# Window attention pass on one core: second norm centred in SBUF, values in the single PSUM bank, 49 weight columns, second MLP product in three parts

## The chip, the cores and the metric

The kernel runs on 1 of the 8 cores of one Trainium2 chip. The metric is device time in microseconds (us). All times are of whole executions of the program on the chip; the profile is one execution under the hardware profiler. The engines are named as in the profile: PE (TensorE; PEld is its weight loads), DVE (VectorE), ACT (ScalarE), POOL (GpSimd) and SP (SyncE, which issues the DMAs). TensorE's clock is granted at one of two levels here, 1.2 and 2.4 GHz; the profile shows the granted share (0.5 or 1).

## The reference

Two residual blocks on x of shape (32, 96, 56, 56), f32: a depthwise 31x31 convolution of the group norm of x, then a vision transformer block on shifted 7x7 windows of the group norm of that.

```python
x = x + conv31x31_depthwise(group_norm(x), weight) + bias_term
x = x + window_block(group_norm(x))

def _ln(x, s, b):
    m = jnp.mean(x, axis=-1, keepdims=True)
    v = jnp.var(x, axis=-1, keepdims=True)
    return (x - m) * jax.lax.rsqrt(v + EPS) * s + b

def _vit(t, ...):                    # t: (windows, 49 tokens, 96), 12 heads of 8
    h = _ln(t, ln1_s, ln1_b)
    q, k, v = h @ wq + bq, h @ wk + bk, h @ wv + bv
    scores = jnp.einsum('nqhd,nkhd->nhqk', q, k) / np.sqrt(dh)
    attn = jax.nn.softmax(scores, axis=-1)
    o = jnp.einsum('nhqk,nkhd->nqhd', attn, v).reshape(N, S, D)
    t = t + o @ wo + bo
    h = _ln(t, ln2_s, ln2_b)
    return t + jax.nn.gelu(h @ w1 + b1) @ w2 + b2
```

The change touches only how the second norm, the values, the product of probabilities and values, and the product with `w2` are placed and ordered.

## The kernel before

`conv_pass` does the first block and writes x1 to DRAM; the change leaves it alone. `window_pass` does the second. Its unit is a **strip**: 8 windows, that is 392 tokens (NT), with the 96 channels on partitions. There are 256 strips (32 images of 8). The pass is a pipeline written out by hand: each engine has one function `step(i, s)` that is unrolled 256 + 9 times, and in one step (one **turn** below) each stage works on another strip: QKV (first norm, q, k, v) on strip n - 2, ATT (scores) on n - 4, SOFT (probabilities) on n - 6, PROJ (attention output and second norm) on n - 7, MLPS on n - 8. The order of an engine's work is the order of the lines of its `step`; semaphores (`S[...]`) tie the engines together. There is no scheduler.

PSUM has eight banks: `ps_s` and `ps_t` two each (scores, transposed scores), `ps_pv` one, `ps_xc` one ("the single bank"), and a ring of two, `ps_ring`. The table `USES` gives the order in which products take the ring's banks; a product may start when the use two places ahead has been read (`wait_bank`, L599). So in the kernel before, the second variance (`var2`) waits for `q_done`, the values (`v`) for `k_done`, and so on.

What PE does in a turn, in order (L1125 to L1190): transposed scores 0 (`below_max`, L1098); the first norm's centring product into `ps_xc` (L1133, L1134); scores 0; transposed scores 1; `times_v` for two window pairs (L1107); `expand` 0 and 1, the first MLP product (L1058 to L1060); scores 1, transposed scores 2, `expand` 2; four transposes of the attention output (L1149); scores 2; the first variance (`spread`, L1066, L1067); the output projection `wo` (L1049); `times_v` for the other two pairs; scores 3; **the centring product of the second norm** into `ps_xc` (L1163, f32); q and k (L1049); transposed scores 3; the transpose of the row maxima (`max_rows`, L1095); **the second variance** as two single-pass products of the squares split in two (`sq2_hi`, `sq2_lo`); **the values** (L1180) into a ring bank; and **the second MLP product** (L1188), nine matmuls, three for each of three blocks of 128 hidden units.

An f32 product is two records in the trace (two weight loads, two matmuls); one in F32R is one record, and where F32R is used an operand is split into a high part and a remainder.

`times_v` multiplies, for each head and window pair, the probabilities as weights with the values as the moving side (two windows of 9 columns: 8 values and a column of ones that yields the denominator). Two window pairs go to the two halves of the partitions. It loads 64 weight columns (`WS`) of which 49 (`TOK`) are tokens; the other 15 are the start of the next head's:

```python
to = ps_pv[WS * odd:WS * odd + WS, ...][:, half, :, h, :]
ins = pe.matmul(to, pt[:, p, at:at + WS], vd[:, m % VR, p, h, :, :], start=True, stop=True,
                skip_group_check=True)
```

The second norm is a chain over three engines: centring product (PE, L1163) into the single bank; two squares (ACT, L848, `sq2` and `sq2_hi`); their difference (DVE, L978, `sq2_lo`); variance (PE); logarithm and exponential (ACT, L827, L832); `h2_hi` and `h2` as product of the single bank with `rstd` (DVE, L1004, L1008); and their difference `h2_lo` (DVE, L1026), which signals `h2_split` and lets `expand` start in the next turn. The single bank is held from the centring product until both products have read it, and the next strip's first norm waits for that (L1130, L1131). On DVE the q and k remainders (L983, L987) stand between L978 and L1004, and the copy of the values (L1014) and the sum `y` (L1021) between L1008 and L1026. POOL splits the hidden units (`mid_high`, `mid_low`: L739, L746), splits the q and k remainders into planes (L788, L792), and adds `y` to the input (L801).

## Time and profile before

| | us |
|---|---|
| median of 3 runs | 5706.78 |
| lowest, highest | 5679.43, 5709.63 |
| the profiled execution, its own time | 5688.4 |
| its span, first to last instruction | 5686.6 |
| PE busy (share of the span) | 5342.2 (94%) |
| DVE, ACT, POOL busy | 3397.2, 3542.0, 3509.3 |
| mean granted clock of TensorE | 0.976 |

How to read it: busy time is summed over instructions, and PE's matmuls are pipelined, so an engine that shows as busy need not be at its peak. The conv pass takes about the first quarter of the span. A row of the groups gives line, engine, operation, output and inputs, shapes (partitions x elements), count, then busy us and mean ns of one, then idle time of the engine just before and what ended it.

### The profile page before, as it was taken

To read this page: it belongs to the slowest core of one execution; us is meant where nothing else is said; L and a number is where in the kernel's file an instruction comes from. 1 tells how busy PE (TensorE), PEld (TensorE's weight loads), DVE (VectorE), ACT (ScalarE), POOL (GpSimd) and SP (SyncE) were. 2 spreads that over 40 slices of the span, in tenths; PEclk is the share of its full clock that TensorE was granted. 3 is DMA by queue.
4 is the path that set the end of the run, shared out by engine and by line. 5 is a ranking of instruction groups with operands and counts; after the bars stand their busy time and mean duration, and the time that the engine had idled before them with its cause. 6 is when DMAs were issued, how large, how long until landed. Compare 5 with 4: busy or idle time off the path is not lost.

```text
span 5686.6 us, 229687 instructions
## 1 busy us (share of the span) xinstructions
PE 5342.2 (94%) x97360; PEld 4217.5 (74%) x97360; DVE 3397.2 (60%) x5850; ACT 3542.0 (62%) x5590; POOL 3509.3 (62%) x4814
## 2 busy tenths in 40 slices
PE   6999999999599999999999999999999999999998
PEld 6999999999466666666666666666666666666665
DVE  2333333433267677677676777776677777777773
ACT  3444444444367777777776777777777777777775
POOL 2222222222367777777777777777777777777774
PEclk9999999999689999999998999999999999999996
DMA  4444444444356666666665666666666666666662
GB/s 125 116 121 120 127 121 120 116 125 104 71 126 140 140 140 140 140 140 140 140 140 127 139 139 140 140 140 140 140 140 140 140 140 140 140 140 140 140 140 47
DMA packets 1099823, 740.58 MB, mean 130 GB/s; under 512 B 465428, under 2 KB 1070708, under 8 KB 1098708
## 3 DMA queue, kind: packets, MB, share of 16 engines
q1 hardware_dynamic: 1069620, 687.18, 53.6%
q0 software_dynamic: 29184, 38.71, 3.2%
q8 instruction: 774, 12.68, 1.0%
q14 instruction: 245, 2.01, 0.1%
HBM read 409.02 MB, written 316.46 MB: 128 GB/s over the span
## 4 chain that ended last, share of the span: by engine, by line
PE 61%; issue 7%; DVE 3%; ACT 3%; POOL 0%; ACTq 0%; DVEq 0%; POOLq 0%
PE ps_pv L1121 14%; PE ps_ring L1188 8%; PE ps_s L1075 5%; PE ps_ring L1058 4%; PE ps_xc L1163 4%; PE ps_ring L1049 4%; PE ps_t L1075 4%; PE ps_ring L1180 4%; PE ps_ring L1066 4%; PE ps_ring L1060 2%; PE ps_ring L1059 2%; DVE b_rest L983 2%; ACT b_sq_hi L848 2%; PE ps_ring L1149 2%; PE ps_ring L1067 2%
## 5 line engine op out<-in xcount | busy, mean ns | idle before, releaser
L940 DVE TENSOR_REDUCE b_mx<-ps_s 113x12 f32<-113x588 f32 x1024 | 783.9, 766 | 200.6 <-PE ps_s L1075 200.4
L1121 PEld LDWEIGHTS ps_pv<-b_vd,b_probs_t 128*64 128x64 f32 x24576 | 771.1, 140 | 164.0 <-issue 155.1
L840 ACT ACTIVATE b_probs_t<-ps_t 128x588 f32<-128x588 f32 x1024 | 667.7, 652 | 303.0 <-PE ps_t L1075 302.9
L225 POOL TENSOR_SCALAR xn<-xin,aff 96x896 f32<-96x896 f32 x192 | 173.4, 903 | 1072.2 <-DVE aff L375 1059.5
L1121 PE MATMUL ps_pv<-b_vd,b_probs_t 128*64 128x18 f32 x24576 | 822.5, 213 | 0.3 <-issue 0.3
L746 POOL TENSOR_TENSOR b_mid_lo<-b_mid,b_mid_hi 128x392 fp32r<-128x392 f32 x768 | 788.9, 1027 | 43.3
L410 PE MATMUL ps_conv<-blocks_hi,toep_hi 128*128 128x288 f32 (+2 forms) x2880 | 667.2, 313 | 0.0
L410 PE MATMUL ps_conv<-blocks_hi,toep_lo 128*128 128x288 f32 (+2 forms) x2880 | 654.4, 309 | 0.0
L410 PE MATMUL ps_conv<-blocks_lo,toep_hi 128*128 128x288 f32 (+2 forms) x2880 | 653.7, 308 | 0.0
L801 POOL TENSOR_TENSOR b_outs<-b_y,b_xs 96x392 f32<-96x392 f32 x256 | 316.7, 1237 | 445.2 <-DVE b_y L1021 445.2
L282 ACT ACTIVATE toep_hi<-toep 128x640 fp32r<-128x640 f32 x288 | 197.2, 749 | 632.9 <-PE ps_conv L410 616.7
L855 ACT ACTIVATE b_mid<-ps_ring,b_cols 128x392 f32<-128x392 f32 x768 | 438.2, 587 | 196.2 <-PE ps_ring L1060 180.5
L827 ACT ACTIVATE b_lg<-ps_ring,b_cols 96x392 f32<-96x392 f32 x512 | 298.4, 583 | 324.8 <-PE ps_ring L1067 321.8
L788 POOL TENSOR_SCALAR b_planes<-b_rest 96x784 bf16<-96x784 f32 x256 | 215.5, 842 | 440.3 <-DVE b_rest L987 440.3
L327 DVE TENSOR_SCALAR conv_sb<-ps_conv,biasb 128x896 f32<-128x896 f32 x96 | 110.5, 1151 | 625.4 <-PE ps_conv L410 625.4
L410 PEld LDWEIGHTS ps_conv<-blocks_hi,toep_lo 128*128 128x128 f32 x2880 | 464.5, 189 | 4.2
L410 PEld LDWEIGHTS ps_conv<-blocks_hi,toep_hi 128*128 128x128 f32 x2880 | 464.4, 189 | 3.9
L410 PEld LDWEIGHTS ps_conv<-blocks_lo,toep_hi 128*128 128x128 f32 x2880 | 464.0, 189 | 4.3
L1075 PEld LDWEIGHTS ps_t<-b_q_st,b_k_st 51*49 51x49 bf16 x24576 | 260.0, 100 | 258.1 <-issue 228.6
L848 ACT ACTIVATE b_sq<-ps_xc 96x392 f32<-96x392 f32 x512 | 252.6, 493 | 312.8 <-PE ps_xc L1163 312.8
L792 POOL TENSOR_TENSOR b_planes<-b_rest,b_planes 96x784 bf16<-96x784 f32 x256 | 432.2, 1688 | 21.3
L739 POOL TENSOR_SCALAR b_mid_hi<-b_mid 128x392 fp32r<-128x392 f32 x768 | 396.5, 516 | 13.0 <-ACT b_mid L855 13.0
(142 smaller groups left out, 12423.3 us busy)
## 6 DMA issues: line engine op xcount, KB each, us to landing
stacked_qk<-b_planes SPq DMA_DIRECT2D x512, 220.5 KB, 2.9
b_q_st<-stacked_qk SPq DMA_DIRECT2D x512, 220.5 KB, 4.3
b_k_st<-stacked_qk SPq DMA_DIRECT2D x512, 220.5 KB, 5.6
toep<-filters_padded SPq DMA_DIRECT2D x96, 936.5 KB, 14.0
stacked_qk<-b_planes SPq DMA_DIRECT2D x512, 147.0 KB, 2.4
stacked_qk<-b_planes SPq DMA_DIRECT2D x512, 73.5 KB, 1.9
b_xs<-x_scratch SPq DMA_DIRECT2D x224, 147.0 KB, 2.8
out<-b_outs SPq DMA_DIRECT2D x224, 147.0 KB, 3.2
```

The costliest lines, as they stand in the source:

```text
L410: ins = pe.matmul(to[:, first // 2:first // 2 + n, y0 * BATCH:y1 * BATCH], taps[:, par, 1 + dy, NDX // 2 + dx, :], data[:, par, first + dx ...
L739: pool.tensor_scalar(mid_hi[:, m, :], mid[:, m, :], 1.0, 0.0, ALU.mult, ALU.add).then_inc(S["mid_high"], 1)
L746: pool.tensor_tensor(mid_lo[:, m, :], mid[:, m, :], mid_hi[:, m, :].bitcast(F32), ALU.subtract).then_inc(S["mid_split"], 1)
L792: pool.tensor_tensor(planes[:, 2, :, :], rest[:, :, :], planes[:, 1, :, :], ALU.subtract).then_inc(S["qk_split"], 1)
L801: pool.tensor_tensor(tokens(outs[:, sl % 2]), windows(y[:, sl % 2, :]), tokens(xs[:, mlps % XS]), ALU.add).then_inc(S["added"], 1)
L840: act.activation(pt[:, p, 0:HEADS * TOK].rearrange("k (e n) -> k e n", e=2), ps_t[:, :, 0:HPAIR * TOK], ACT.Exp, scale=float(DH) ** -0.5). ...
L848: act.activation(dst[:, :], ps_xc[0:C, 0:NT], ACT.Square, scale=scale).then_inc(S[done], 1)
L855: act.activation(mid[:, m, :], bank(i, s, use)[:, 0:NT], ACT.Gelu_apprx_tanh, bias=cols[:, B1 + m:B1 + m + 1]).then_inc(S["gelu_done"], 1)
L940: dve.tensor_reduce(mx[0:rows_q, :].rearrange("q (e m p) -> q e m p", e=2, p=PAIRS)[:, :, :, p], ps_s[0:rows_q, :, 0:HPAIR * TOK].rearrang ...
L1075: ins = pe.matmul(dst[WS * w:WS * w + TOK, e, h * TOK:(h + 1) * TOK], a[k, m % SR, h, t], b[k, m % SR, h, t], start=True, stop=True, skip_ ...
L1121: ins = pe.matmul(to, pt[:, p, at:at + WS], vd[:, m % VR, p, h, :, :], start=True, stop=True, skip_group_check=True)
L1188: ins = pe.matmul(bank(i, s, "w2")[0:C, 0:NT], w[:, m, :], src[:, m, :], start=(m == 0 and n == 0), stop=(m == NM - 1 and n == 2))
```

## The change

- Second norm: PE now forms the **mean** of `t1` (a product with a constant matrix of 1/96) in a ring bank (`mean2`), and DVE subtracts it from `t1` into a new tile `xc2` in SBUF. One square (ACT, of `xc2`) takes the place of two, `sq2_lo` and its DVE instruction are gone, and the variance is one f32 product with `ones_f`. `h2_hi` and `h2` are products of `xc2` and `rstd`, both in SBUF. In DVE's order `xc2` stands ahead of the fourth row maximum.
- Values: their product goes into the single bank `ps_xc`, which holds the first norm's centred values until `h1` is made, and the copy out of it now comes ahead of `h2_hi` on DVE. The next strip's first norm waits for that copy (`v_done`) in place of `h2_high` and `h2_done`. The ring's order changes: `mean2` takes a place ahead of q, `v` has none; the product with `w2` now follows `var2`.
- `times_v` loads 49 weight columns and writes 49 rows. `ps_pv` is set to 1 once at the start, so that the rows between are defined.
- The product with `w2` is `contract`, called for one block of hidden units at a time at the start of the **next** turn: before transposed scores 0, after them, and after the first norm's product.
- On PE the values come ahead of `var2`. On ACT the fourth exponential comes ahead of the second norm's logarithm.

The file of the changed kernel holds two definitions of `window_pass`; the second replaces the first and alone runs, so its lines carry numbers some 650 higher. The diff is that of the function that runs (declarations left out).

```diff
                 ("var1", QKV, "lg1", 1, 1), ("wo", PROJ, "t1_done", 1, 1),
-                ("q", QKV, "q_done", 1, 1), ("k", QKV, "k_done", 1, 1),
-                ("var2", PROJ, "lg2", 1, 1), ("v", QKV, "v_done", 1, 1),
+                ("mean2", PROJ, "xc2", 1, 1), ("q", QKV, "q_done", 1, 1),
+                ("k", QKV, "k_done", 1, 1), ("var2", PROJ, "lg2", 1, 1),
                 ("w2", MLPS, "y_done", 1, 1)]
...
                 if proj is not None:
-                    square(i, proj, sq2, "xc2", "sq2", "sq2_split")
-                if proj is not None:
-                    square(i, proj, sq2_hi, "xc2", "sq2_high", "sq2_split", used="var2")
+                    square(i, proj, sq2, xc2[:, :], "xc2", "sq2", ("var2",))
                 if qkv is not None:
...
                     act.activation(planes[:, 0, 1, :], bank(i, s, "k")[0:C, 0:NT], ACT.Copy).then_inc(S["k_high"], 1)
+                exps(i, soft, 3)
                 if proj is not None:
...
                     inv_std(proj, "lg2", "rstd2")
-                exps(i, soft, 3)
             steps(act, step)
...
             dve.memset(ps_t[:, :, :], 0.0)
+            dve.memset(ps_pv[:, :], 1.0)
             dve.memset(cols[:, :], 0.0).then_inc(S["zeroed_v"], 1)
...
                                              ALU.mult).then_inc(S["h1_done"], 1)
-                row_max(i, att, 3)
                 if proj is not None:
-                    dve.wait_ge(S["sq2_high"], proj + 1)
-                    dve.wait_ge(S["sq2"], proj + 1)
-                    dve.tensor_tensor(sq2_lo[:, :], sq2[:, :], sq2_hi[:, :].bitcast(F32), ALU.subtract).then_inc(
-                        S["sq2_split"], 1)
+                    dve.wait_ge(S["mean2"], proj + 1)
+                    after(dve, i, "sq2", proj)
+                    after(dve, i, "h2_high", proj)
+                    after(dve, i, "h2_done", proj)
+                    dve.tensor_tensor(xc2[:, :], t1[:, proj % 2, :], bank(i, s, "mean2")[0:C, 0:NT],
+                                      ALU.subtract).then_inc(S["xc2"], 1)
+                row_max(i, att, 3)
                 if qkv is not None:
...
                         S["mx_rest"], 1)
-                if proj is not None:
-                    dve.wait_ge(S["rstd2"], proj + 1)
-                    after(dve, i, "w1_ps", NM * proj)
-                    after(dve, i, "h2_split", proj)
-                    dve.tensor_tensor(h2_hi[:, :], ps_xc[0:C, 0:NT], rstd[:, :], ALU.mult).then_inc(S["h2_high"], 1)
-                if proj is not None:
-                    dve.wait_ge(S["rstd2"], proj + 1)
-                    after(dve, i, "h2_split", proj)
-                    dve.tensor_tensor(h2[:, :], ps_xc[0:C, 0:NT], rstd[:, :], ALU.mult).then_inc(S["h2_done"], 1)
                 if qkv is not None:
...
                         ins = dve.tensor_copy(vd[r, qkv % VR, :, :, a, 0:DH],
-                                              bank(i, s, "v")[r, 0:PAIRS * C].rearrange("t (p h d) -> t p h d", p=PAIRS,
+                                              ps_xc[r, 0:PAIRS * C].rearrange("t (p h d) -> t p h d", p=PAIRS,
                                                                                         d=DH))
                     ins.then_inc(S["v_done"], 1)
+                if proj is not None:
+                    dve.wait_ge(S["rstd2"], proj + 1)
+                    after(dve, i, "w1_ps", NM * proj)
+                    after(dve, i, "h2_split", proj)
+                    dve.tensor_tensor(h2_hi[:, :], xc2[:, :], rstd[:, :], ALU.mult).then_inc(S["h2_high"], 1)
+                if proj is not None:
+                    dve.wait_ge(S["rstd2"], proj + 1)
+                    after(dve, i, "h2_split", proj)
+                    dve.tensor_tensor(h2[:, :], xc2[:, :], rstd[:, :], ALU.mult).then_inc(S["h2_done"], 1)
                 if mlps is not None:
...
                         p = 2 * half + odd
-                        to = ps_pv[WS * odd:WS * odd + WS, 0:PAIRS * HEADS * VA].rearrange(
+                        to = ps_pv[WS * odd:WS * odd + TOK, 0:PAIRS * HEADS * VA].rearrange(
                             "q (a w h d) -> q a w h d", a=2, w=2, d=VA)[:, half, :, h, :]
-                        ins = pe.matmul(to, pt[:, p, at:at + WS], vd[:, m % VR, p, h, :, :], start=True, stop=True,
+                        ins = pe.matmul(to, pt[:, p, at:at + TOK], vd[:, m % VR, p, h, :, :], start=True, stop=True,
                                         skip_group_check=True)
...
 
+            def contract(i, s, n, m):
+                if n is None:
+                    return
+                if m == 0:
+                    wait_bank(pe, i, s, "w2")
+                pe.wait_ge(S["mid_split"], NM * n + m + 1)
+                for k, (w, src) in enumerate(((w2_hi, mid_hi), (w2_lo, mid_hi), (w2_hi, mid_lo))):
+                    ins = pe.matmul(bank(i, s, "w2")[0:C, 0:NT], w[:, m, :], src[:, m, :],
+                                    start=(m == 0 and k == 0), stop=(m == NM - 1 and k == 2))
+                if m == NM - 1:
+                    ins.then_inc(S["w2_ps"], 1)
+
             def step(i, s):
                 qkv, att, soft, proj, mlps = (strip(i, s, x) for x in (QKV, ATT, SOFT, PROJ, MLPS))
+                held = strip(i, s, MLPS + 1)
+                contract(i, s - 1, held, 0)
                 below_max(i, soft, 0)
+                contract(i, s - 1, held, 1)
                 if qkv is not None:
                     pe.wait_ge(S["t0_split"], qkv + 1)
-                    after(pe, i, "h2_done", qkv - (PROJ - QKV))
-                    after(pe, i, "h2_high", qkv - (PROJ - QKV))
+                    after(pe, i, "v_done", qkv)
 
...
                               stop=True).then_inc(S["xc1"], 1)
+                contract(i, s - 1, held, 2)
                 scores(i, att, 0)
...
                     pe.wait_ge(S["t1_done"], proj + 1)
-
-                    pe.wait_ge(S["h1_done"], qkv + 1 if qkv is not None else BATCH * B)
-                    pe.matmul(ps_xc[0:C, 0:NT], cc("center", C), t1[:, proj % 2, :], start=True,
-                              stop=True).then_inc(S["xc2"], 1)
+                    product(i, s, "mean2", cc("average", C), t1[:, proj % 2, :], C, "mean2")
                 if qkv is not None:
...
                 max_rows(i, s, att)
-                if proj is not None:
-                    spread(i, s, proj, "var2", sq2_hi, sq2_lo, "sq2_split", "var2")
                 if qkv is not None:
-                    wait_bank(pe, i, s, "v")
+                    pe.wait_ge(S["h1_done"], qkv + 1)
                     for p in range(PAIRS):
...
                             t = slice((2 * p + w) * TOK, (2 * p + w + 1) * TOK)
-                            ins = pe.matmul(bank(i, s, "v")[WS * w:WS * w + TOK, p * C:(p + 1) * C], h1[0:C, t],
+                            ins = pe.matmul(ps_xc[WS * w:WS * w + TOK, p * C:(p + 1) * C], h1[0:C, t],
                                             wv[:, :], start=True, stop=True, skip_group_check=True)
                     ins.then_inc(S["v_ps"], 1)
-                if mlps is not None:
-                    wait_bank(pe, i, s, "w2")
-                    for m in range(NM):
-                        pe.wait_ge(S["mid_split"], NM * mlps + m + 1)
-                        for n, (w, src) in enumerate(((w2_hi, mid_hi), (w2_lo, mid_hi), (w2_hi, mid_lo))):
-                            ins = pe.matmul(bank(i, s, "w2")[0:C, 0:NT], w[:, m, :], src[:, m, :],
-                                            start=(m == 0 and n == 0), stop=(m == NM - 1 and n == 2))
-                    ins.then_inc(S["w2_ps"], 1)
+                if proj is not None:
+                    pe.wait_ge(S["sq2"], proj + 1)
+                    product(i, s, "var2", ones_f[:, :], sq2[:, :], C, "var2")
             steps(pe, step)
 
+
```

The first place is the end of a turn on PE and the start of the next, before: the second norm's centring product (from `b_t`), q and k, transposed scores 3, the transpose of the row maxima, the variance (two rows), the values, and the first three of nine matmuls with `w2` (the other six read alike).

```order
L1163 MATMUL ps_xc<-b_t,b_const 96x392
L1049 MATMUL ps_ring<-b_h,b_wqk 96x392 x2
L1075 MATMUL ps_t<-b_q_st,b_k_st 49x49 x24
L1095 MATMUL ps_s<-b_const,b_mx 48x113
L1066 MATMUL ps_ring<-b_sq_hi,b_ones 96x392
L1067 MATMUL ps_ring<-b_sq_lo,b_ones 96x392
L1180 MATMUL ps_ring<-b_wv,b_h 49x96 x8
L1188 MATMUL ps_ring<-b_mid_hi,b_w_hi 96x392
L1188 MATMUL ps_ring<-b_mid_hi,b_w_lo 96x392
L1188 MATMUL ps_ring<-b_mid_lo,b_w_hi 96x392
```

And of the change:

```order
L1697 MATMUL ps_ring<-b_t,b_const 96x392
L1697 MATMUL ps_ring<-b_h,b_wqk 96x392 x2
L1723 MATMUL ps_t<-b_q_st,b_k_st 49x49 x24
L1743 MATMUL ps_s<-b_const,b_mx 48x113
L1838 MATMUL ps_xc<-b_wv,b_h 49x96 x8
L1697 MATMUL ps_ring<-b_sq,b_ones_f 96x392
L1780 MATMUL ps_ring<-b_mid_hi,b_w_hi 96x392
L1780 MATMUL ps_ring<-b_mid_hi,b_w_lo 96x392
L1780 MATMUL ps_ring<-b_mid_lo,b_w_hi 96x392
L1723 MATMUL ps_t<-b_q_st,b_k_st 49x49 x24
L1780 MATMUL ps_ring<-b_mid_hi,b_w_hi 96x392
```

The values moved ahead of the variance and into `ps_xc`; the variance is one row; three matmuls with `w2` stand on each side of transposed scores 0 (`ps_t`), and three more follow the first norm's product.

The second place is DVE from `h1` (its first row) to `h2_lo`, before:

```order
L972 SCALAR_TENSOR_TENSOR b_h<-ps_xc,b_rstd 96x392
L940 TENSOR_REDUCE b_mx<-ps_s 113x12
L978 TENSOR_TENSOR b_sq_lo<-b_sq,b_sq_hi 96x392
L983 TENSOR_TENSOR b_rest<-ps_ring,b_planes 96x392
L987 TENSOR_TENSOR b_rest<-ps_ring,b_planes 96x392
L994 CAST b_mx_planes<-ps_s 48x98
L998 TENSOR_TENSOR b_mx_rest<-ps_s,b_mx_planes 48x98
L1004 TENSOR_TENSOR b_h_hi<-ps_xc,b_rstd 96x392
L1008 TENSOR_TENSOR b_h<-ps_xc,b_rstd 96x392
L1014 COPY b_vd<-ps_ring 49x48x8 x2
L1021 SCALAR_TENSOR_TENSOR b_y<-ps_ring,b_cols,b_t 96x392
L1026 TENSOR_TENSOR b_h_lo<-b_h,b_h_hi 96x392
```

And of the change:

```order
L1618 SCALAR_TENSOR_TENSOR b_h<-ps_xc,b_rstd 96x392
L1625 TENSOR_TENSOR b_xc<-b_t,ps_ring 96x392
L1586 TENSOR_REDUCE b_mx<-ps_s 113x12
L1631 TENSOR_TENSOR b_rest<-ps_ring,b_planes 96x392
L1635 TENSOR_TENSOR b_rest<-ps_ring,b_planes 96x392
L1642 CAST b_mx_planes<-ps_s 48x98
L1646 TENSOR_TENSOR b_mx_rest<-ps_s,b_mx_planes 48x98
L1653 COPY b_vd<-ps_xc 49x48x8 x2
L1661 TENSOR_TENSOR b_h_hi<-b_xc,b_rstd 96x392
L1665 TENSOR_TENSOR b_h<-b_xc,b_rstd 96x392
L1669 SCALAR_TENSOR_TENSOR b_y<-ps_ring,b_cols,b_t 96x392
L1674 TENSOR_TENSOR b_h_lo<-b_h,b_h_hi 96x392
```

`xc2` (named `b_xc`) stands ahead of the row maximum in place of `sq2_lo` behind it; the copy of the values (`b_vd`) moved ahead of the two products, which now read `b_xc`.

## Rows read from the trace of the kernel before

**Rows 1.** The page: busy us, and the granted clock in 40 slices

```profile
PE 5342.2 (94%) x97360; PEld 4217.5 (74%) x97360; DVE 3397.2 (60%) x5850; ACT 3542.0 (62%) x5590; POOL 3509.3 (62%) x4814
...
PEclk9999999999689999999998999999999999999996
```

**Rows 2.** By stretch: us, busy of PE, PEld, DVE, ACT, POOL; PEclk; DMA

```profile
1480.00:1628.00 148.00, 93.70 (x1442) 60.54 (x1442) 57.06 (x106) 64.19 (x94) 74.12 (x87) 0.54 0.47 103
3133.00:5590.00 2457.00, 2331.00 (x52872) 1678.43 (x52871) 1718.44 (x3099) 1753.88 (x2940) 1905.21 (x2646) 1.00 0.65 140
3033.00:3046.60 13.60, 13.60 (x166) 9.01 (x164) 5.29 (x10) 6.36 (x11) 7.93 (x12) 0.50 0.44 94
```

**Rows 3.** Line L1095, from 3133 and from 1628 us: durations, first and last start

```profile
L1095 PE MATMUL ps_s<-b_const,b_mx x155: 277/279/280, 3133.3 to 5571.8; 113*48 113x113 f32 x155
...
L1095 PE MATMUL ps_s<-b_const,b_mx x249: 277/279/381, 1632.3 to 5571.8; 113*48 113x113 f32 x125
```

**Rows 4.** Waits from 3133 to 5590 us: total, times, longest

```profile
PE ps_ring L1066 <- DVE b_rest L983: 105.2, 155, 0.9
```

**Rows 5.** PE in order of time, 3004 to 3028 us: start, us from first start

```profile
3010.47 0.39 PE L1066 MATMUL ps_ring<-b_sq_hi,b_ones 96*96 96x392 f32 x1 [0.66 <-DVE b_rest L983]
...
3010.96 0.87 PE L1180 MATMUL ps_ring<-b_wv,b_h 96*49 96x96 f32 x16
3011.76 0.42 PE L1188 MATMUL ps_ring<-b_mid_hi,b_w_hi 128*96 128x392 f32 x1
3012.02 0.34 PE L1188 MATMUL ps_ring<-b_mid_hi,b_w_lo 128*96 128x392 f32 x1
...
3013.55 0.34 PE L1075 MATMUL ps_t<-b_q_st,b_k_st 51*49 51x49 bf16 x24
...
3014.34 0.34 PE L1075 MATMUL ps_s<-b_k_st,b_q_st 48*49 48x49 bf16 x24
...
3014.96 1.58 PE L1121 MATMUL ps_pv<-b_vd,b_probs_t 128*64 128x18 f32 x48
3016.47 0.45 PE L1058 MATMUL ps_ring<-b_h_hi,b_w_hi 96*128 96x392 f32 x1
...
3022.93 0.87 PE L1163 MATMUL ps_xc<-b_t,b_const 96*96 96x392 f32 x2
3023.64 1.48 PE L1049 MATMUL ps_ring<-b_h,b_wqk 97*96 97x392 f32 x4
3025.05 0.35 PE L1075 MATMUL ps_t<-b_q_st,b_k_st 51*49 51x49 bf16 x24
```

**Rows 6.** PE in order of time in a stretch at the lower clock level

```profile
3039.80 2.75 PE L1121 MATMUL ps_pv<-b_vd,b_probs_t 128*64 128x18 f32 x48
```

**Rows 7.** Groups from 3133 to 5590 us, and lines L978 and L1026 (min/median/max)

```profile
L1121 PEld LDWEIGHTS ps_pv<-b_vd,b_probs_t 128*64 128x64 f32 x14880 | 460.3, 138 | 97.1 <-issue 91.6
...
L1180 PEld LDWEIGHTS ps_ring<-b_wv,b_h 96*49 96x49 f32 x2480 | 103.5, 124 | 43.9 <-DVE b_rest L987 43.9
...
L889 ACT ACTIVATE b_planes<-ps_ring 96x392 bf16<-96x392 f32 x155 | 76.3, 492 | 8.4
...
L978 DVE TENSOR_TENSOR b_sq_lo<-b_sq,b_sq_hi x239: 561/891/1164, 1710.6 to 5492.2; 96x392 fp32r<-96x392 f32 x120
...
L1026 DVE TENSOR_TENSOR b_h_lo<-b_h,b_h_hi x240: 548/552/554, 1700.8 to 5498.2; 96x392 fp32r<-96x392 f32 x120
```

**Rows 8.** DVE in order of time, same turn

```profile
3008.95 0.89 DVE L978 TENSOR_TENSOR b_sq_lo<-b_sq,b_sq_hi 96x392 fp32r<-96x392 f32 x1 [1.02 <-ACT b_sq_hi L848]
...
3010.24 0.55 DVE L987 TENSOR_TENSOR b_rest<-ps_ring,b_planes 96x392 f32<-96x392 f32 x1
...
3012.31 0.56 DVE L1004 TENSOR_TENSOR b_h_hi<-ps_xc,b_rstd 96x392 fp32r<-96x392 f32 x1 [1.07 <-ACT b_rstd L832]
```

**Rows 9.** POOL in order of time, same turn

```profile
3008.39 1.03 POOL L746 TENSOR_TENSOR b_mid_lo<-b_mid,b_mid_hi 128x392 fp32r<-128x392 f32 x1
...
3011.88 1.68 POOL L792 TENSOR_TENSOR b_planes<-b_rest,b_planes 96x784 bf16<-96x784 f32 x1
```

603 lines of the change are left out of this document (589 added, 14 removed).

## The prediction

> **What bounds the kernel now.** I read the page first, then busy time by stretch, then the waits, then one turn of the window pass engine by engine.
>
> The page shows TensorE (PE) busy for 94% of the span, the other engines about 60%, and the clock at its upper level nearly everywhere [rows 1]. The stretches say where the time lies: after a conv pass that the change does not touch there are some 148 us in which the window pass fills up at the lower clock level, then some 3960 us of even turns [rows 2]. The 155 row-maximum transposes from 3133.3 to 5571.8 us give the length of a turn: 2438.5 / 154 = 15.83 us; 249 such turns are counted in the even part [rows 3]. Only what a turn of PE is made of can move the time. Its one real wait is that of the first matmul of the second variance: 105.2 us over 155 turns, 0.68 us a turn, released by VectorE's (DVE's) q remainder [rows 4], ahead of which `sq2_lo` stands on DVE. So PE is bound by its own work for 15.15 us and by a chain for 0.68 us. The reader should look in the PE turn at start-to-start distances, not at durations, because matmuls overlap [rows 5].
>
> **Part 1, 49 weight columns in `times_v`.** The product runs 96 records a turn (24 matmuls of two records, twice). At the upper level (2.4 GHz) 48 of them take 1.58 us from the first start to the last end and 1.51 us to the next start (3014.96 to 3016.47), at the lower level (1.2 GHz) 2.75 us [rows 5, 6]. The difference is 1.17 us or 24.4 ns a record, and a cycle is 0.417 ns longer: 59 of a record's 75 cycles (1.51 us / 48 x 2.4 GHz) follow the clock. The moving side has 18 columns, the weights 64, so I take the weights for the limit. Scaled to 49 columns, 59 x 15/64 = 14 cycles or 5.8 ns go: 0.55 us a turn. The load rows say much the same: 138 ns for 64 f32 columns, 124 for 49 [rows 7], 14 ns less; two column tiles run side by side, so 48 x 14 = 0.67 us. I take 0.60. Bounds: 0 (if a record is set by something that both widths share) and 1.34 (if the loads of both tiles come one after another). The Trainium skill (TensorE: Matmul & The Clock Gate, LDWEIGHTS) gives a load as its columns divided by 1.2 GHz, whatever the rows: 12.5 ns less here. By that alone the term would be an estimated 0.60 side by side and 1.20 in series.
>
> **Part 2, the second variance.** Two single-pass products (0.49 us, 3010.47 to 3010.96) become one f32 product. The same shape in f32 takes 0.71 us (3022.93 to 3023.64) [rows 5]: +0.22 us. The mean product replaces the centring product, f32 of the same shape: 0. The value matmuls keep their form: 0.
>
> **Part 3, the second MLP product in three parts.** The nine matmuls take 1.79 us as one block [rows 5]. A first dense record after a group of small products costs 0.26 us to the next start (3011.76 to 3012.02); the other eight take 0.19 each. But the first part now follows the variance directly and the third follows the first norm's product directly, so there are as many borders as before: 0 (bounds -0.1 and +0.2).
>
> **Part 4, the wait.** Now the square needs one ScalarE (ACT) instruction, not two and a DVE split (891 ns [rows 7]), and PE's variance stands behind the value matmuls. From the start of k's product: 0.70 to its end in the stream, transposed scores 0.28, transpose 0.28 [rows 3], values 0.80, so the variance comes at +2.06. The q remainder that frees its bank comes before the k remainder, which starts at about +1.5 (k lands after 0.87, ACT's copy 0.49, and signals [rows 7]), and `sq2` is earlier still. So 0.68 us goes. What is late next: k's product must wait for the bank of the mean, and that for `xc2` on DVE. Mean product 0.87 to landing, subtraction 0.56, signals some 0.19: 1.62 us after the mean's start, where k's turn would come at 1.41 [rows 5, 8]. I charge 0.21 us (bounds 0 and 0.4). DVE has finished `h1` by then; the row maximum queued behind `xc2` moves back 0.6 us, and the transpose that needs it still comes after it.
>
> **Part 5, DVE's two products from SBUF.** `h2_hi` and `h2` now read `xc2` and `rstd`, both in SBUF, where one operand was in PSUM. The rows show what that can cost: `sq2_lo`, two SBUF operands, takes 891 ns in the middle case; `h2_lo`, the same kind, 552 [rows 7]. The instance in the turn explains it: GpSimd (POOL) runs `mid_lo` from 3008.39 to 3009.42, `sq2_lo` starts at 3008.95 and ends 0.42 us after POOL does [rows 8, 9]. The Trainium skill has this as a rule (SBUF — State Buffer, Who interferes with whom): a DVE instruction with two SBUF inputs excludes a GpSimd one that reads SBUF. It agrees with those rows and speaks against this change.
>
> Priced from rows: POOL's last q/k plane ends 3.32 us after the k remainder starts (3010.24, 3013.56) [rows 8, 9], here 2.76 after the variance starts. `h2_hi` would be ready 1.84 + 0.32 = 2.16 after it (3012.31 less 3010.47, plus the longer product) and is held to 2.76, ending at 3.18. `h2`, `y` and `h2_lo` follow in 1.60, so `h2_split` is at 4.78. PE meets it after 0.71 (variance) + 2.58 (three parts, transposed scores, first norm) + 0.62 (two more groups of small products) + 1.21 (`times_v`, shortened) = 5.12 [rows 5]. So 0.2 us is left after the signal, and the cost is 0; if that cover goes, each 0.1 us costs 25 us in all. `y` must come before `h2_lo` and needs the third part, which ends at 3.29, before its place. POOL's busy time is 1905 / 155 = 12.3 us a turn [rows 2] and fits. ACT's exponential now stands ahead of the logarithm, in ACT's idle time; it frees the first transposed scores of the next turn sooner. SP's DMAs are the same in number and order and hang on POOL events that move with the turn: 0.
>
> **Sum.** -0.60 + 0.22 + 0 - 0.68 + 0.21 = -0.85 us, so turns of 14.98 us. Times 249: -212 us. The fill at the lower level and the drain gain perhaps 5 us more, since PE is not the bound there. The low-clock stretches inside the even part (13.6 us from 3033 is one [rows 2]) I leave as they are. Profiled 5688.4 - 217 = 5471; the median of the three runs is 5706.78, 18 above the profiled execution, so I put the median at **5485 us**. The executions shown differ by 0.5%, about what a measurement can tell from no change.
>
> **Rivals.**
> 1. *More than that.* k's wait is absorbed and one or two borders close up: turns of 14.7, 5420 us. For it: the transpose's 0.28 is a duration, its stream time is likely shorter. Chance 0.17.
> 2. *The new chain takes PE's place.* The 0.2 us before `h2_split` is not there: POOL's 1.69 us subtraction holds both DVE products, `h2_lo` slips 0.3 to 0.5 us, and the first MLP product waits every turn. Turns of 15.3 to 15.5, about 5595 us. For it: the middle one of 239 `sq2_lo` took 891 ns where the shortest took 561 [rows 7]. Against it: the sum above has that hold in it. Chance 0.15. The rule of the Trainium skill cited above bears on this rival and on no other.
> 3. *49 columns cost what 64 did.* The record is set by its tile, not by its columns: turns of 15.58 and 5635 us. Against it: 59 cycles that follow the clock, and the 124 ns load. Chance 0.05.
> 4. *Slower: the granted clock.* The upper level is lost in the even part. In the even part the level fell too, once for the 13.6 us from 3033 [rows 2] and the rows do not tell why; the change thins `times_v` and breaks up the densest block. Work in `times_v` takes 1.74 times as long at the lower level (2.75 / 1.58 [rows 5, 6]), so each us there loses 0.43. The 217 us are gone at about 500 us of low clock, an eighth of the even part; at a quarter the kernel takes 5910 us. For it: those falls. Against it: the same matmul work in less time, with the largest gap closed. Chance 0.08.
>
> My forecast has the remaining 0.55.
>
> **Numbers.** The range goes from the better case, with the load term a little above mine, to the second rival: 5390 to 5610. It leaves out the third, the fourth and the far end of the first. Faster by over 0.5% are the forecast and rivals 1 to 3, less a little for several small misses together: 0.89; within 0.5%: 0.03; slower: 0.08.
>
> **What would show it.** Right: even turns of 14.9 to 15.1 us; 48 `times_v` records in 1.2 us; the loads near 124 ns; no wait on the variance; a wait of 0.2 us on k's product released by `xc2`; `h2_hi` well above 562 ns. Wrong: `times_v` still at 1.5 us; a wait of the first MLP product on `h2_lo`; the clock digits at 7 or 8 through the window pass.

## The result, and the profile after

The changed kernel takes 5451.02 us (median of 4 executions, 5418.92 to 5457.99), the kernel before 5708.20 beside it: a ratio of 0.9548 (95% interval 0.9524 to 0.9573). The forecast of 5485 was 34 us too high and the range held the time. The sum behind it was right only as a sum: two of its errors nearly cancel (norm and split better by 0.27 us a turn, a wait on a DMA worse by 0.31), and its opening account of what bounds the kernel before was wrong.

The page of the changed kernel: busy us, and the granted clock in 40 slices, as [rows 1].

```profile
PE 5203.4 (96%) x97360; PEld 4039.8 (74%) x97360; DVE 3400.9 (62%) x5852; ACT 3474.8 (64%) x5334; POOL 3510.0 (64%) x4814
...
PEclk9999999999859999999999999999999999999999
```

PE's busy time fell by 139 us, the span by 239; of the others only ACT (one square less a turn) has less to do. The row-maximum transpose, which [rows 3] counted, over the whole run, before and after (durations, first to last start):

```profile
L1095 PE MATMUL ps_s<-b_const,b_mx x256: 277/279/395, 1548.1 to 5611.1; 113*48 113x113 f32 x128
```
```profile
L1743 PE MATMUL ps_s<-b_const,b_mx x256: 278/278/395, 1547.2 to 5394.7; 113*48 113x113 f32 x128
```

The 255 turns went from 4063.0 to 3847.5 us, 215.5 less; what follows the last one (before, span 5686.6) went from 75.5 to 53.3 us. That second gain of 22 us goes with the granted clock, 0.59 before and 0.90 now at the end (columns as in [rows 2], before, then after); in the other runs of the changed kernel below this tail takes 53 to 70 us:

```profile
5611.00:5686.60 75.60, 56.65 (x560) 38.23 (x550) 18.41 (x35) 33.17 (x47) 25.67 (x36) 0.59 0.06 12
```
```profile
5394.70:5448.00 53.30, 38.27 (x546) 25.88 (x546) 17.59 (x34) 30.82 (x42) 25.62 (x36) 0.90 0.08 17
```

In what follows a turn is measured in two ways, both from starts of one PE instruction: the **mean** over the part from 3133 to 5300 us, in which the kernel before keeps the upper clock level, as count, first and last start of the row-maximum transpose; and the **median** of the last 246 distances, after the fill, which a few late turns do not move. The kernel before: (5286.8 - 3133.3) / 136 = 15.83 mean, 15.80 median. The changed kernel, first and last start and count, and its waits on PE and on PE's weight loads in the same part (total, times, longest), where before had [rows 4]:

```profile
L1743 PE MATMUL ps_s<-b_const,b_mx x144: 278/278/279, 3145.9 to 5292.7; 113*48 113x113 f32 x144
```
```profile
PE ps_t L1723 <- DMA b_q_st<-row_maxima: 36.2, 52, 1.5
```
```profile
PEld ps_t L1723 <- DMA b_q_st<-row_maxima: 67.7, 91, 1.9
```

The mean is 2146.8 / 143 = 15.01 us, the shortest turns take 14.68, and the median is 14.73. The wait on DVE's q remainder is gone. In its place stands one that the prediction did not have: the transposed scores, or the load of their weights, wait for a DMA in 91 of 144 turns. PE in order of time in such a turn (lines answer to [rows 5]):

```profile
3207.06 0.90 PE L1697 MATMUL ps_ring<-b_sq,b_ones_f 96*96 96x392 f32 x2
...
3209.50 0.34 PE L1723 MATMUL ps_t<-b_q_st,b_k_st 51*49 51x49 bf16 x24 [1.00 <-DMA b_q_st<-row_maxima]
...
3211.86 1.28 PE L1769 MATMUL ps_pv<-b_vd,b_probs_t 128*49 128x18 f32 x48
3213.07 0.44 PE L1706 MATMUL ps_ring<-b_h_hi,b_w_hi 96*128 96x392 f32 x1
...
3219.10 0.90 PE L1697 MATMUL ps_ring<-b_t,b_const 96*96 96x392 f32 x2
3219.84 1.78 PE L1697 MATMUL ps_ring<-b_h,b_wqk 97*96 97x392 f32 x4
3221.54 0.35 PE L1723 MATMUL ps_t<-b_q_st,b_k_st 51*49 51x49 bf16 x24
```

The 48 records of `times_v` take 1.21 us to the next start, not 1.51; no wait stands ahead of the variance; q and k take 1.70 us, not 1.41, since k waits for `xc2`.

Where the DMA comes from is in the chain of waits that ends at that transpose (start, us, what, pieces in order of time):

```profile
3194.68 0.71 issue
3195.38 0.55 DVE b_h L1665
...
3196.67 1.24 POOL b_outs L1448
...
3198.26 0.38 POOL b_mx_planes L1461
3198.65 0.30 SPq L1327
...
3199.47 1.69 SPq L1339
...
3203.67 5.79 DMA b_q_st<-row_maxima
```

The issue of 0.71 us is spent in `h2_hi`, which takes 0.93 us here where an unheld one takes 0.55, beside POOL's subtraction of a q/k plane. `y` follows on it, `outs` waits for `y`, the maxima's split waits behind `outs` on POOL, their store behind the split, and their loads stand last in SP's queue, behind the q and k loads, with 5.79 us to land. What differs from turn to turn stands on SP: `h2_hi` takes 0.91 to 0.93 us in nine turns of ten, but the issue of the store of `out` (L1339) takes 1.69 us in this turn and 0.52 in the next. `outs` on POOL, one turn later:

```profile
3212.19 1.23 POOL L1448 TENSOR_TENSOR b_outs<-b_y,b_xs 96x392 f32<-96x392 f32 x1 [2.46 <-DVE b_y L1669]
```

POOL idles 2.46 us ahead of `outs`. The maxima that it could split lie ready: DVE makes `mx_rest` at 3207.17 in 0.25 us.

Is the landing later than before? Counted from the row-maximum transpose, as medians over the turns from 1660 to 5280 us, it is not. `outs` starts after 5.59 us before and 5.33 now, and the maxima have landed after 17.2 us before and 17.3 now. What moved is the place of transposed scores 0 of the next turn: 19.8 us before, 17.1 without a wait now (a turn of 14.69 and 2.38 more, where it was 15.80 and 4.01). So a slack of 2.6 us has become a lack of 0.2: 1.1 us went with the shorter turn, 1.6 with what PE has between the two.

### The profile page after: what moved, and what is told of

The parts are those of the page before. It is cut to its first block, busy times and chain, and to the rows that moved or that the text cites. A ratio compares the mean times of both kernels' runs of the same rounds, so it can differ in the third digit from the quotient of the medians.

```text
span 5448.0 us, 229437 instructions
## 1 busy us (share of the span) xinstructions
PE 5203.4 (96%) x97360; PEld 4039.8 (74%) x97360; DVE 3400.9 (62%) x5852; ACT 3474.8 (64%) x5334; POOL 3510.0 (64%) x4814
## 4 chain that ended last, share of the span: by engine, by line
PE 44%; DMA 10%; SPq 8%; POOL 3%; issue 3%; DVE 2%; ACT 2%; DVEq 0%; ACTq 0%; POOLq 0%
PE ps_ring L1697 12%; DMA b_q_st<-row_maxima 10%; PE ps_pv L1769 7%; PE ps_ring L1780 5%; SPq L1347 4%; PE ps_s L1723 3%; PE ps_t L1723 3%; PE ps_ring L1706 3%; PE ps_xc L1838 2%; POOL b_outs L1448 2%; PE ps_ring L1708 2%; PE ps_ring L1707 2%; SPq L1339 2%; SPq L1333 1%; PE ps_ring L1812 1%
## 5 line engine op out<-in xcount | busy, mean ns | idle before, releaser
L1769 PEld LDWEIGHTS ps_pv<-b_vd,b_probs_t 128*49 128x49 f32 x24576 | 612.2, 127 | 161.0 <-issue 151.9
L1769 PE MATMUL ps_pv<-b_vd,b_probs_t 128*49 128x18 f32 x24576 | 663.0, 200 | 0.2 <-issue 0.2
L1501 ACT ACTIVATE b_mid<-ps_ring,b_cols 128x392 f32<-128x392 f32 x768 | 424.2, 585 | 165.6 <-PE ps_ring L1708 162.0
L1723 PEld LDWEIGHTS ps_t<-b_q_st,b_k_st 51*49 51x49 bf16 x24576 | 272.9, 99 | 301.6 <-issue 182.5
L1697 PE MATMUL ps_ring<-b_h,b_wqk 97*96 97x392 f32 x1024 | 443.1, 516 | 27.5 <-DVE b_h L1618 7.3
L1723 PE MATMUL ps_t<-b_q_st,b_k_st 51*49 51x49 bf16 x24576 | 369.5, 187 | 67.6 <-DMA b_q_st<-row_maxima 65.7
## 6 DMA issues: line engine op xcount, KB each, us to landing
stacked_qk<-b_planes SPq DMA_DIRECT2D x512, 220.5 KB, 3.1
b_q_st<-stacked_qk SPq DMA_DIRECT2D x512, 220.5 KB, 4.4
b_k_st<-stacked_qk SPq DMA_DIRECT2D x512, 220.5 KB, 5.6
toep<-filters_padded SPq DMA_DIRECT2D x96, 936.5 KB, 13.8
```

What stands on the lines that cost most here:

```text
L1501: act.activation(mid[:, m, :], bank(i, s, use)[:, 0:NT], ACT.Gelu_apprx_tanh, bias=cols[:, B1 + m:B1 + m + 1]).then_inc(S["gelu_done"], 1)
L1697: pe.matmul(bank(i, s, use)[0:rows, 0:NT], w, src, start=True, stop=True).then_inc(S[done], 1)
L1723: ins = pe.matmul(dst[WS * w:WS * w + TOK, e, h * TOK:(h + 1) * TOK], a[k, m % SR, h, t], b[k, m % SR, h, t], start=True, stop=True, skip_ ...
L1769: ins = pe.matmul(to, pt[:, p, at:at + TOK], vd[:, m % VR, p, h, :, :], start=True, stop=True, skip_group_check=True)
```

## The experiments

All edits are in the `window_pass` that runs. Two theories were to be told apart: that the kernel before is bound by PE's own stream and one wait (the prediction), and that it is bound by a **loop** over POOL, DVE and ACT, which PE only takes part in. No edit leaves work out. The kernel before took 5700 us (5699.97, 5701.02 and 5700.88) beside the three groups of runs, and 5708 beside the change, so 8 us of a difference from the change's 5451 can be the group's.

### The 49 columns alone, in the kernel before

```diff
-                        ins = pe.matmul(to, pt[:, p, at:at + WS], vd[:, m % VR, p, h, :, :], start=True, stop=True,
+                        ins = pe.matmul(to, pt[:, p, at:at + TOK], vd[:, m % VR, p, h, :, :], start=True, stop=True,
```

> The kernel before with only the 49 weight columns and 49 rows in times_v. Theory (the weight columns limit a record, nothing else in this turn is near): 48 records go by in 1.21 us, not 1.51; even turns fall from 15.83 to 15.23 us; the wait of the second variance stays at 0.68 us; about 5708 - 150 = 5558 us. Rival (a record is set by its tile): 1.51 us and 5708 us. Second rival (the chain of the norm or a DMA takes the freed time): records at 1.21 us but a turn above 15.4.

Measured: 5669.32 us, ratio 0.9945 (0.9926 to 0.9965). The turn stays as it was, 15.79 (median). PE in order of time, its waits, and `sq2_lo` on DVE (min/median/max) in this run:

```profile
3209.68 1.28 PE L1122 MATMUL ps_pv<-b_vd,b_probs_t 128*49 128x18 f32 x48
3210.90 0.35 PE L1076 MATMUL ps_s<-b_k_st,b_q_st 48*49 48x49 bf16 x24
3211.61 0.87 PE L1164 MATMUL ps_xc<-b_t,b_const 96*96 96x392 f32 x2 [0.36 <-DVE b_h L973]
...
3215.25 0.39 PE L1067 MATMUL ps_ring<-b_sq_hi,b_ones 96*96 96x392 f32 x1 [0.97 <-DVE b_rest L984]
```
```profile
PE ps_ring L1067 <- DVE b_rest L984: 125.1, 137, 1.2
PE ps_xc L1164 <- DVE b_h L973: 47.2, 129, 0.6
```
```profile
L979 DVE TENSOR_TENSOR b_sq_lo<-b_sq,b_sq_hi x137: 561/1182/1436, 3134.2 to 5290.9; 96x392 fp32r<-96x392 f32 x137
```

The columns save their 0.30 us per 48 records (1.22 to the next start), 0.60 a turn, and PE loses all of it: 0.36 us at the centring product, for `h1` (the single bank), and 0.23 more at the variance (125.1 / 137 = 0.91 for 0.68). `sq2_lo` takes 291 ns longer at the median than in [rows 7], since it starts sooner and ends 0.43 us after POOL's `mid_lo` as ever. PE's stream did not set the turn. The 31 us are therefore no gain in the even turn. The two profiled executions differ by 17.6 us, 14 of them in those 246 turns although their median moved by 0.01, so in late turns; why these cost less here stays open.

### The change with 64 columns

> The change with 64 weight columns again. Theory (PE's own turn is 14.69 us, and the mean of 15.08 comes from transposed scores 0 waiting for the row maxima's DMA, which is late by the clock of the other engines, not of PE): PE's own turn is 15.29 us, the DMA wait nearly gone, even turns about 15.33, so only 62 us slower than the change, 5513 us. Rival (the wait is DMA contention and stays whatever PE does): turns of 15.68, 5600 us.

Measured: 5554.42 us, ratio 0.9734 (0.9681 to 0.9787). Median turn 15.29. So in the change the columns are worth 103 us, where they were worth 31 before; against the 150 us of 0.60 us a turn the rest goes into the DMA wait, which is shorter here (13.0 us on PE in 26 turns, where the change has 36.2 in 52).

### The second MLP product in one block again

```diff
-                contract(i, s - 1, held, 0)
+                for m in range(NM):
+                    contract(i, s - 1, held, m)
                 below_max(i, soft, 0)
-                contract(i, s - 1, held, 1)
...
-                contract(i, s - 1, held, 2)
```

> The change with the nine matmuls of the second MLP product in one block again, ahead of transposed scores 0. Theory (the split brought transposed scores 0 forward by 1.2 us, into the landing of the row maxima): the DMA wait disappears, PE's own turn stays 14.7, about 5451 - 95 = 5356 us. Rival (the split pays, because it lets the exponential and the first norm start earlier or keeps the clock up): slower than the change, a new wait of ACT or of expand, above 5451 us.

Measured: 5414.35 us, ratio 0.9495 (0.9451 to 0.9538), **37 us faster than the change** by the medians. The two intervals overlap, and one of the change's four executions (5418.92) is as fast as these; the traces bear the difference out, with a mean turn of 14.88 for 15.01, 32 us over 249 turns. PE in order of time, and the exponential on ACT:

```profile
3207.47 0.34 PE L1723 MATMUL ps_t<-b_q_st,b_k_st 51*49 51x49 bf16 x24
...
3208.27 0.34 PE L1723 MATMUL ps_s<-b_k_st,b_q_st 48*49 48x49 bf16 x24
3208.61 0.34 PE L1723 MATMUL ps_t<-b_q_st,b_k_st 51*49 51x49 bf16 x24
```
```profile
3207.90 0.66 ACT L1487 ACTIVATE b_probs_t<-ps_t 128x588 f32<-128x588 f32 x1 [0.72 <-PE ps_t L1723]
```

The transposed scores 0 stand behind nine dense matmuls, not three, so the maxima have landed: PE's wait on them is 0.7 us in all, and 2.6 on its weight loads. But the median turn is 14.83, and not 14.69: transposed scores 1 now start 0.34 us after scores 0 (3208.27 to 3208.61), where the change has 0.18 (3211.38 to 3211.56). They write `ps_t`, which the exponential of transposed scores 0 reads until 3208.56; with the split this exponential has more of PE's work to run beside (2.06 us from transposed scores 0 to 1, here 1.14). So the split gains 0.14 us a turn and loses more by moving the transposed scores 0 into the landing of the maxima: they stand 18.3 us after the row-maximum transpose here, 17.1 in the change.

### The maxima's split ahead of `outs` on POOL, in the change

```diff
+                if att is not None:
+                    pool.wait_ge(S["mx_rest"], att + 1)
+                    pool.tensor_scalar(mx_planes[:, 1, :, :], mx_rest[:, :, :], 1.0, 0.0, ALU.mult, ALU.add).then_inc(
+                        S["mx_mid"], 1)
...
                 if mlps is not None:
                     sl, img = mlps % B, mlps // B
                     pool.wait_ge(S["y_done"], mlps + 1)
```

(The subtraction that makes `mx_split` moves with it; both leave their places behind `outs`.)

> The change with the two POOL instructions that split the row maxima moved ahead of the sum into outs, so that they no longer queue behind y. Theory (the row maxima's load is late because their split waits on POOL for y, which waits for the third part of the product): the load is issued some 3 us earlier, the wait of transposed scores 0 disappears, even turns 14.7, about 5356 us. Rival (SP's own queue or the DMA engines hold the load): the split is earlier but the landing is not, and the time stays near 5451 us.

Measured: 5362.47 us, ratio 0.9403 (0.9361 to 0.9445), 88 us below the change. PE's wait on the DMA is 0.3 us in all, and 2.1 on its weight loads. Row-maximum transposes from 3133 to 5300 us:

```profile
L1743 PE MATMUL ps_s<-b_const,b_mx x148: 278/278/279, 3132.8 to 5294.4; 113*48 113x113 f32 x148
```

Mean turn 2161.6 / 147 = 14.705, so the DMA wait cost the change 0.31 us a turn, 77 us over 249 turns. This is the cleanest of the comparisons: no instruction is added or taken away, two move within one queue. The maxima land 15.5 us after the transpose, not 17.3.

### The same move in the kernel before, and with 49 columns

> The kernel before, with POOL's two instructions that split the row maxima moved ahead of the sum into outs. Theory (before is not bound by PE but by a loop: y, then 10.1 us of POOL work up to its last mid_lo, which holds sq2_lo by the shared SBUF port, then the q remainder, variance, h2, y; 5.7 us): 0.62 us of POOL work leaves the loop, sq2_lo is no longer held (560 ns), the wait of the variance falls from 0.68 to about 0.4 us, even turns 15.5, about 5700 - 75 = 5625 us. Rival (PE and the norm's own chain bind, POOL has slack): turns stay at 15.8, 5700 us.

> The same with the 49 weight columns too. Theory (the 49 columns were worth only 31 us in the kernel before because the POOL loop took the rest, and the wait of the centring product for h1 0.36 us of it): turns of 15.2 to 15.25, about 5555 us, so the columns are worth some 70 us here. Rival (something in PE's own stream or the h1 chain alone eats the columns' gain): about 5600 us or more, no better than 30 us below the run without the columns.

Measured: 5672.07 us, ratio 0.9940 (0.9920 to 0.9961), and 5638.96, ratio 0.9883 (0.9858 to 0.9907). Median turns 15.64 and 15.58. PE's wait on the variance in the second of them (that on `h1` is 46.2 us in 126 turns):

```profile
PE ps_ring L1067 <- DVE b_rest L984: 93.3, 130, 1.0
```

The move alone shortens the kernel before by 28 us and its turn by 0.16, although no transfer was waited for there: POOL's time between `outs` and `mid_lo` is in the loop. The theory was right in kind and too large in size: 15.64 where 15.50 was forecast, and `sq2_lo` still takes 0.73 us at the median, not 0.56. The second forecast (5555, the columns worth 70) was missed clearly, and the rival's number came out: the columns add 33 us. The turn is only 0.06 shorter, 14 us; the profiled execution without them also spent 116 us of its even part at the lower clock level, with them 68. The same two waits as in the first experiment take the rest. That `sq2_lo` and the single bank close the loop is read from these waits; the next run removes both together, and none parts them.

### The new norm and the values alone

The change with 64 columns and one block: what is left is Part 2, Part 4 and Part 5.

> The change without 49 columns and without the split: the norm centred in SBUF and the values in the single bank alone. Theory (this part breaks the POOL loop and the wait of the variance): PE's own turn 15.29 + 0.14, no DMA wait, turns 15.43, about 5575 us. Rival (the norm alone gains little, the gain comes from the combination): above 5650 us.

Measured: 5589.31 us, ratio 0.9802 (0.9781 to 0.9822), median turn 15.43. PE in order of time, in the kernel before and in this run:

```profile
3209.55 0.34 PE L1075 MATMUL ps_s<-b_k_st,b_q_st 48*49 48x49 bf16 x24
3209.96 0.87 PE L1163 MATMUL ps_xc<-b_t,b_const 96*96 96x392 f32 x2
...
3212.36 0.28 PE L1095 MATMUL ps_s<-b_const,b_mx 113*48 113x113 f32 x1
3213.28 0.39 PE L1066 MATMUL ps_ring<-b_sq_hi,b_ones 96*96 96x392 f32 x1 [0.65 <-DVE b_rest L983]
...
3213.78 0.87 PE L1180 MATMUL ps_ring<-b_wv,b_h 96*49 96x96 f32 x16
```
```profile
3213.23 0.35 PE L1723 MATMUL ps_s<-b_k_st,b_q_st 48*49 48x49 bf16 x24
3213.50 0.90 PE L1697 MATMUL ps_ring<-b_t,b_const 96*96 96x392 f32 x2
3214.24 1.77 PE L1697 MATMUL ps_ring<-b_h,b_wqk 97*96 97x392 f32 x4
3215.95 0.35 PE L1723 MATMUL ps_t<-b_q_st,b_k_st 51*49 51x49 bf16 x24
...
3217.23 0.90 PE L1697 MATMUL ps_ring<-b_sq,b_ones_f 96*96 96x392 f32 x2
...
3218.15 0.34 PE L1780 MATMUL ps_ring<-b_mid_hi,b_w_lo 128*96 128x392 f32 x1
```

The turn came out as forecast. This gives the pieces: the kernel before with this part 112 us less; then, with the loop gone, the columns 175 us more (5589 to 5414, of which 0.59 us a turn, 147 us, are turns); the split then costs 37. Alone, in the kernel before, the columns gave 31.

### The mean product ahead of scores 3

```diff
-                scores(i, att, 3)
                 if proj is not None:
                     pe.wait_ge(S["t1_done"], proj + 1)
                     product(i, s, "mean2", cc("average", C), t1[:, proj % 2, :], C, "mean2")
+                scores(i, att, 3)
```

This is a try at k's wait, on top of the maxima first.

> The change with the maxima split first on POOL (5362 us in e4) and the mean product ahead of scores 3 on PE. Theory (k's product waits 0.3 us for xc2; 0.28 us more of cover removes that, one more border costs 0.08): PE's own turn 14.47 us, about 5362 - 55 = 5307 us. Rival (the mean then waits for t1 or its bank, and the wait moves): 5362 us or more.

Measured: 5343.99 us, ratio 0.9368 (0.9351 to 0.9385): the best version of this study, 107 us below the change. PE in order of time:

```profile
3204.16 0.90 PE L1697 MATMUL ps_ring<-b_t,b_const 96*96 96x392 f32 x2
3204.99 0.35 PE L1723 MATMUL ps_s<-b_k_st,b_q_st 48*49 48x49 bf16 x24
3205.27 1.56 PE L1697 MATMUL ps_ring<-b_h,b_wqk 97*96 97x392 f32 x4
3206.76 0.35 PE L1723 MATMUL ps_t<-b_q_st,b_k_st 51*49 51x49 bf16 x24
```

q and k take 1.49 us, 0.21 less than in the change. The gain over the maxima first is 18 us where 55 were forecast, and in turns 0.13 (14.56 for 14.69), not 0.22, since the mean product now takes 0.83 us to the next start, not 0.74: it follows on `times_v` and is followed by scores, a border more on each side.

### A spare copy on POOL

One copy of 96 columns a turn, of a tile that nobody uses, in the kernel before and in the change with the maxima first.

```diff
+                pool.tensor_copy(spare[:, 0, :], spare[:, 1, :])
                 mid_high(mlps, 0, i)
```

> The kernel before, with one more GpSimd instruction a turn: a copy of 96 columns of a spare tile ahead of the first mid_hi. Nobody waits for its result. Theory: the turn of the kernel before (median 15.80 us) is closed by a loop in which GpSimd stands from outs to the last mid_lo, so the turn grows by most of the copy's length d (the trace will give d, I guess 0.3 us): median turn 15.80 + 0.8 d to 15.80 + d, about 16.05 us, and the time 5701 + 249 x 0.25 = 5763 us. Rival (the prediction's reading): the turn is TensorE's own work and a wait that GpSimd does not reach; GpSimd is busy 12.3 us of 15.8 and swallows the copy: turn 15.80, time 5701 us.

> The changed kernel with GpSimd's work on the maxima moved ahead of outs (5362 us, median turn 14.69), with the same spare copy a turn. Theory: here TensorE's own stream sets the turn and GpSimd has idle time, so the copy costs nothing: turn 14.70 to 14.75 us, time 5362 to 5375 us. Rival: GpSimd's loop is still as tight as TensorE's stream and the copy costs its length here too: turn 14.95, time 5425 us.

Measured: 5750.85 us, ratio 1.0083 (1.0052 to 1.0114), and 5374.26, ratio 0.9424 (0.9395 to 0.9453). POOL in order of time around the copy, and PE's row-maximum transposes, in the first:

```profile
3201.36 0.26 POOL L767 COPY b_spare<-b_spare 96x96 f32<-96x96 f32 x1
3201.60 0.51 POOL L741 TENSOR_SCALAR b_mid_hi<-b_mid 128x392 fp32r<-128x392 f32 x1
```
```profile
L1098 PE MATMUL ps_s<-b_const,b_mx x134: 278/278/279, 3144.3 to 5287.4; 113*48 113x113 f32 x134
```

The copy puts POOL's next instruction off by 0.24 us and the median turn goes from 15.80 to 16.01: 0.21, times 249 is 52 us, and 50 were measured. In the change with the maxima first the median turn is 14.69 with the copy and without it. So POOL was in the loop that set the turn before, with 12.3 of 15.8 us busy [rows 2], and sets nothing in the change once the maxima are out of the way of `outs`. (The change as it is was not run with the copy.)

### The maxima's loads ahead of the q and k loads on SP, in the change

```diff
+                n = strip(i, s, MAXR)
+                if n is not None:
+                    sp.wait_ge(mx_written[n % 2], 16 * (n // 2 + 1))
...
                 n = strip(i, s, STK)
                 if n is not None:
                     sp.wait_ge(stk_written[n % 2], WRITES * (n // 2 + 1))
```

> The changed kernel as built, with one edit on SyncE: the two loads of row_maxima are issued ahead of the four q and k loads, not behind them. Theory: what the change lost is the landing of these loads, some 5.8 us after an issue that stands behind 2 us of other issues; issued 2 us sooner, and with nothing large ahead of them, they land before the transposed scores and the wait on the DMA is gone: median turn 14.69 us, time 5365 us, as with GpSimd's order changed. Rival 1: the landing is late because the maxima's split on GpSimd is late, and the store's own landing (1.4 us) and SyncE's wait for it now delay the q and k loads: the wait halves, 5410 us. Rival 2: the q and k loads now come late for the scores: 5450 us or more.

Measured: 5433.89 us, ratio 0.9515 (0.9465 to 0.9565). The median turn is 14.70, as forecast, and no wait on the maxima is left: they land 12.4 us after the row-maximum transpose. But the time is 69 us above the forecast. Two things took it. First, PE waits a little for k's loads, now last in the queue:

```profile
PEld ps_s L1723 <- DMA b_k_st<-stacked_qk: 9.0, 17, 1.3
```

Second, the granted clock: by stretch, the first of this run's seven falls and the sum of them, then a part with none.

```profile
1932.20:1952.70 20.50, 20.50 (x244) 13.46 (x243) 8.88 (x17) 9.14 (x15) 9.96 (x13) 0.51 0.50 108
...
sum 126.50, PE 126.50 PEld 81.83 DVE 52.03 ACT 56.49 POOL 62.12; mean PE 18.07 PEld 11.69 DVE 7.43 ACT 8.07 POOL 8.87
```
```profile
3000.00:4000.00 1000.00, 986.41 (x23085) 691.14 (x23081) 752.08 (x1355) 746.93 (x1218) 833.17 (x1159) 1.00 0.70 150
```

Where the clock holds, PE gets through 23085 matmuls in 1000 us, 0.4% fewer than with POOL's order changed (23189); over 249 turns that is 17 us, so an estimate of 5380. The seven falls last 126.5 us, and hold 1656 matmuls (244, 191, 329, 191, 192, 243, 266), which take 72 us at the other rate: 55 us lost, 5435 in all. The profiled execution took 5437.6. The other three fit: with mean granted clocks of 0.971, 0.981 and 0.975 they took 5448, 5401 and 5430, where the four with POOL's order changed had 0.984 to 0.986. Why the clock falls with this order and hardly with the other is not settled. In the 60 us ahead of each fall stands one wait or two of PE on k's loads, which come some 127 us apart on the whole (17 in 2167 us); but the stretch from 3300 to 3360 us has two of them and no fall behind it, and the change has five times as many DMA waits and few falls.

## Why the prediction was right, and where it was not

**What bounds the kernel before: wrong.** "PE is bound by its own work for 15.15 us and by a chain for 0.68 us" and "only what a turn of PE is made of can move the time" do not hold. A copy on POOL that nobody waits for made the turn 0.21 us longer, and 0.60 us less work on PE made it no shorter. The median of 15.80 is a loop, and its two parts add up to it: from the end of POOL's last `mid_lo` to `outs` 5.69 us (3009.42 to 3015.11 in the turn of [rows 8, 9]), and from `outs` to the end of the next last `mid_lo` 10.11 (3202.13 to 3212.24). In order: POOL's last `mid_lo` ends; `sq2_lo`, held by it, ends 0.42 us later [rows 8, 9]; the q remainder, the variance, logarithm and exponential, `h2_hi`, `h2`, the value copies and `y` on DVE follow; then `outs`, for which POOL waits 1.55 us in all of the 137 turns, and POOL's ten microseconds, without a gap, to `mid_lo` again. The prediction had that hold before its eyes and used it for `h2_hi` alone. The end of a wait that comes every turn was a reason to follow the chain once around.

**Part 1, 49 columns.** The term of 0.60 us was right: 0.30 for each 48 records, and loads of 126 ns for 138. The estimate from the page of the Trainium skill (TensorE: Matmul & The Clock Gate, LDWEIGHTS), 12.5 ns a load and 0.60 us side by side, agrees with the trace in the difference; for the whole load of 64 columns the page's rule gives an estimated 53 ns, and the row has 138. The step "two side by side" was a guess that came out: 48 records in 1.51 us are 31 ns apiece, so more than four loads of 138 ns overlap, and why their difference still counts as by twos no run shows. What was wrong is the silent claim that the term can be had by itself.

**Part 2, the f32 variance.** +0.22 was forecast. From the variance to the second matmul with `w2` it is 0.92 us (3217.23 to 3218.15), where two passes and the first dense record took 0.50 and 0.26: +0.16, as the product with `w2` now follows a dense matmul and pays no border.

**Part 3, the split.** 0 was forecast, with bounds to either side. It is -0.14 by itself (14.83 in one block, 14.69 split with the maxima out of the way; the exponential gets more time) and brings the transposed scores forward by 1.1 us (six dense matmuls of 0.18), which is what lets the landing be late.

**Part 4, the waits.** The variance's wait of 0.68 is gone with its 0.03 of signal, and so is a gap of 0.14 ahead of the mean product, which had to wait for `h1` (0.41 from scores 3 to the centring product before, 0.27 now). k's wait is 0.30, and 0.21 was charged. With Part 2 these are -0.14 - 0.71 + 0.16 + 0.30, about -0.39 (the 0.71: maxima to variance 0.92 before, maxima to values 0.21 now); the run with the new norm and the values alone shows -0.38 (15.804 to 15.429) where the prediction had -0.25.

**Part 5, DVE's two products from SBUF.** The hold came as computed: the middle one of 145 `h2_hi` takes 923 ns where [rows 7] have 552 for an unheld one, and the first MLP product never waited for `h2_lo`. The trace agrees with the rule of the Trainium skill (SBUF — State Buffer, Who interferes with whom), by which a DVE instruction with two SBUF inputs contends with a GpSimd one that reads SBUF. The step that failed is the one on SP: "hang on POOL events that move with the turn: 0". The POOL events did move with the turn: `outs` and the landing come 5.3 and 17.3 us after the row-maximum transpose, where they came 5.6 and 17.2 us after it. What the term left out is the reader of these loads: transposed scores 0 moved forward by 2.7 us against them and met the landing, 0.31 us a turn. Moving PE's product back, the maxima's split forward on POOL, or the loads forward on SP each removes the wait, as three of the runs show. The hold of `h2_hi` adds its 0.37 us to the same chain, but no run takes it away, so its share in the wait is not shown.

**Sum.** In place of -0.60 + 0.22 - 0.68 + 0.21 = -0.85 the runs have -0.59 (columns) - 0.38 (norm and values) - 0.14 (split) = -1.11, then +0.31 for the DMA: -0.80, and 15.83 - 15.01 = 0.82 by the traces. The 5 us for fill and drain were 23, 22 of them in the drain, with the higher clock there. Of the 34 us by which the forecast was too high, 21 are in the profiled execution (5471 against 5449.8), most of it that drain; the other 13 are the distance kept between profiled and median time, which was 1 us here.

**Rivals.** *More than that* has the turn of 14.7 that the change reaches without the DMA wait. *The new chain takes PE's place* did not happen: PE waits for a DMA behind the same POOL queue, not for `h2_lo`. *49 columns cost what 64 did* is refuted. *The granted clock* was a matter of a few stretches in the change.

## What to carry to other kernels

When PE shows one regular wait in every turn, follow its chain back until it meets itself. If it does, an engine at 78% can set the turn, and taking work off PE need not shorten the turn until the loop is cut (here it did not); a dummy instruction of known length on the suspected engine tells in one run. When a step is moved forward, list every transfer that it waits for, with the place of its issue in the queue, and not only the engines. In an in-order queue, put what another engine waits for ahead of what waits for another engine.
